# Projected keys copied out of PSUM once as f32 by ScalarE, with the remainder made by GpSimd

## What is computed

```python
kv = cond @ wkv.T + bkv                       # cond: 1500 x 256 per sequence
k, v = jnp.split(kv, 2, axis=-1)              # 16 heads of 16
attn = softmax(einsum('bnhd,bmhd->bhnm', q, k) * scale)
o = einsum('bhnm,bmhd->bnhd', attn, v)
out = qdq(o) @ qdq(wp).T + bp
```

## Time and profile before

| | us |
|---|---|
| median of 3 runs (lowest to highest) | 856.81 (855.29 to 857.29) |
| the profiled execution: its own time | 855.01 |
| the profiled execution: span from first to last instruction | 853.2 |
| PE busy | 772.5 (91%) |
| DVE busy | 638.0 (75%) |
| ACT busy | 510.9 (60%) |
| POOL busy | 296.4 (35%) |

### The profile page before, as it was taken

The page is one execution under the profiler, slowest core; times in us unless marked ns, Lnnn a source line. Parts: engine busy times, 40 slices in busy tenths (PEclk is TensorE's granted clock), DMA queues, the critical chain, the costliest instruction groups (busy, mean ns, idle before and its releaser), DMA issues.

```text
span 853.2 us, 30042 instructions
## 1 busy us (share of the span) xinstructions
PE 772.5 (91%) x12379; PEld 582.2 (68%) x12379; DVE 638.0 (75%) x1234; ACT 510.9 (60%) x1084; POOL 296.4 (35%) x366
## 2 busy tenths in 40 slices
PE   4689989999998999999899999999897799999996
PEld 2356666566666666666666666666665589999995
DVE  5877667777787879778787878877774735688887
ACT  2346666566576666666665666566654543777772
POOL 4263226232812461264217322722350003134232
PEclk9899999999999999999999999999999999999999
DMA  7366655454555556555555554645476975766653
GB/s 228 90 176 177 183 131 162 132 160 138 168 145 155 165 152 183 160 152 163 165 153 148 153 172 136 178 129 159 138 200 173 306 259 160 225 190 207 213 135 98
DMA packets 91380, 143.27 MB, mean 168 GB/s; under 512 B 11423, under 2 KB 79583, under 8 KB 87918
## 3 DMA queue, kind: packets, MB, share of 16 engines
q1 hardware_dynamic: 87742, 136.74, 53.8%
q0 software_dynamic: 3504, 4.62, 2.8%
HBM read 101.60 MB, written 39.68 MB: 166 GB/s over the span
## 4 chain that ended last, share of the span: by engine, by line
PE 62%; DVE 13%; ACT 10%; DMA 7%; issue 5%; SPq 2%; POOL 1%; DVEq 0%; POOLq 0%; ACTq 0%
PE ps L1655 14%; PE ps L1648 11%; PE ps L1967 7%; PE ps L1729 7%; PE ps L1707 6%; DVE negmax L522 4%; PE ps L2001 3%; DMA sums<-y_sb,g_token 3%; DMA k_st<-k_dram 3%; ACT pT L1437 3%; ACT k_front L1410 3%; PE ps L1671 3%; DVE k_front L516 3%; PE ps L1772 2%; PE ps L1988 2%
## 5 line engine op out<-in xcount | busy, mean ns | idle before, releaser
L522 DVE TENSOR_REDUCE negmax<-ps 112x1 f32<-112x1500 f32 x121 | 207.4, 1714 | 36.7 <-PE ps L1671 36.6
L1437 ACT ACTIVATE pT<-ps 125x448 f32<-125x448 f32 x384 | 195.6, 546 | 26.6 <-PE ps L1707 23.0
L1261 POOL TENSOR_TENSOR ctx_lo<-ctx_raw,ctx_hi 128x250 f16<-128x250 f32 x188 | 119.3, 666 | 177.8 <-DVE ctx_hi L507 177.8
L1707 PE MATMUL ps<-qbd,k_st 97*128 97x112 f16 x1536 | 128.2, 215 | 16.9 <-ACT pT L1437 8.9
L1707 PEld LDWEIGHTS ps<-qbd,k_st 97*128 97x128 f16 x1536 | 91.5, 99 | 73.1 <-ACT pT L1437 20.2
L1393 ACT COPY v_sb<-ps 125x512 f32<-125x512 f32 x96 | 56.3, 587 | 82.4 <-PE ps L1655 82.4
L516 DVE SCALAR_TENSOR_TENSOR k_front<-ps,bk_sb,k_front 128x500 f16<-128x500 f32 x80 | 58.8, 735 | 61.1 <-ACT k_front L1410 61.1
L1729 PE MATMUL ps<-pT,v_sb 125*17 125x56 f32 x6144 | 92.4, 216 | 8.5 <-issue 8.4
L1729 PEld LDWEIGHTS ps<-pT,v_sb 125*17 125x17 f32 x6144 | 80.6, 99 | 27.8 <-issue 16.1
L1410 ACT ACTIVATE k_front<-ps,bk_sb 128x500 f16<-128x500 f32 x80 | 54.3, 678 | 61.4 <-PE ps L1648 61.4
L1655 PE MATMUL ps<-wkv_hi,ctx_hi 128*125 128x256 f16 x384 | 76.4, 280 | 10.7 <-DVE k_front L516 9.2
(11 more groups left out here) (263 smaller groups left out, 1495.6 us busy)
## 6 DMA issues: line engine op xcount, KB each, us to landing
k_st<-k_dram SPq DMA_DIRECT2D x288, 125.0 KB, 3.0
w_sb<-w SPq DMA_DIRECT2D x25, 1024.0 KB, 5.0
ctx_raw<-ctx_T SPq DMA_DIRECT2D x48, 500.0 KB, 4.1
k_dram<-k_front SPq DMA_DIRECT2D x80, 250.0 KB, 2.7
xs<-zeros SPq DMA_DIRECT2D x28, 260.0 KB
w_sb<-w SPq DMA_DIRECT2D x8, 512.0 KB, 5.2
k_dram<-k_back SPq DMA_DIRECT2D x16, 250.0 KB, 2.9
xg<-xs SPq DMA_DIRECT2D x21, 130.0 KB, 4.1
```

Source lines behind the costliest of these rows:

```text
L522: V.tensor_reduce(negmax[0:QW], ps[0:QW, BANK_S:BANK_S + CHUNKS, 0:MC], AX.XY, ALU.max, negate=True).then_inc(max_done, 1)
L1261: last = nc.gpsimd.tensor_tensor(ctx_lo[:, k, c2, a], ctx_raw[:, k, c2, a], ctx_hi[:, k, c2, a], ALU.subtract)
L1437: nc.scalar.activation(pT[0:MT, (PAIRS * b + p) % 3, TPC * g:TPC * g + TPC], ps[0:MT, BANK_T + n % 2, 0:TPC * QW].rearrange("p (t n) -> p ...
L1707: last = mm(ps[:, BANK_T + n % 2, QW * i:QW * i + QW], k_st[:, j, p, a:a + P], qbd[:, j, p].rearrange("p h s -> p (h s)"), start=True, sto ...
```

## The change

ScalarE now reads the PSUM bank once, adds the bias and writes the key as f32 into one of two new buffers, `k_full`. This instruction frees the bank. A second ScalarE instruction rounds it to f16 (it waits for the first one's semaphore, `unit_out`). GpSimd subtracts in two halves of 250 columns and raises `k_lo_done`, for which the store waits; for the first batch alone the subtraction stays on VectorE. The six two-part buffers become four, used in turn, and ScalarE waits before it writes a buffer again. `load_keys` of unit 6 is issued directly behind its own store (its completion is waited for) and no longer behind unit 8's store. GpSimd's `iteration` gets a `k_lo_step` for every key unit, and three waits in `qbd_step` change.

```diff
             def unit_step(b, par, u):
                 c, g = UNIT[u]
                 if g in KEYS:
-                    i = key_place(c, g)
-                    dve.wait_ge(unit_done, UNITS * b + u + 1)
-
-                    dve.wait_ge(k_hi_done, len(KEY_UNITS) * b + KEY_UNITS.index(u) + 1)
-                    V.scalar_tensor_tensor(k_two[i][:, 1], ps[:, BANK_KV, 0:MC], bk_sb[:, g:g + 1], k_two[i][:, 0],
-                                           ALU.add, ALU.subtract).then_inc(unit_out, 1)
+                    n = key_number(b, u)
+
+                    dve.wait_ge(k_hi_done, n + 1)
+                    V.tensor_tensor(k_two[:, n % 4, 1], k_full[n % 2], k_two[:, n % 4, 0], ALU.subtract).then_inc(k_lo_done, 1)
...
-                    if units_on:
-                        for u in unit_slots(slot):
-                            unit_step(b + 1, 1 - j, u)
...
                         if u == 0:
                             load_keys(b - 1, j, KEY_UNITS[-1])
-                        else:
+                        elif u != 8:
                             load_keys(b, 1 - j, KEY_UNITS[KEY_UNITS.index(u) - 1])
+                        if u == 6:
+                            load_keys(b, 1 - j, u)
...
+            def k_lo_step(b, u):
+
+                n = key_number(b, u)
+                pool.wait_ge(k_hi_done, n + 1)
+                if n == len(KEY_UNITS):
+                    pool.wait_ge(k_lo_done, n)
+                for half in range(2):
+                    a = slice(MC // 2 * half, MC // 2 * half + MC // 2)
+                    last = nc.gpsimd.tensor_tensor(k_two[:, n % 4, 1, a], k_full[n % 2][:, a], k_two[:, n % 4, 0, a], ALU.subtract)
+                last.then_inc(k_lo_done, 1)
...
             def iteration(it, t_before):
-                ctx_lo_step(2 * it + 1, 1, 1)
+                b = 2 * it + 1
+                ctx_lo_step(b, 1, 1)
+                k_lo_step(b, 0)
+                k_lo_step(b, 2)
                 if it > 1:
                     scatter(it - 2)
                 if it > 0:
                     pool.wait_ge(b_oq_done, it)
                 kbd_step(it + 1)
...
             def k_hi_step(b, u):
 
                 c, g = UNIT[u]
-                i = key_place(c, g)
-                if b > 0:
-
-                    act.wait_ge(*stored(b - 1, u))
+                n = key_number(b, u)
                 act.wait_ge(unit_done, UNITS * b + u + 1)
-                nc.scalar.activation(k_two[i][:, 0], ps[:, BANK_KV, 0:MC], ACT.Identity,
-                                     bias=bk_sb[:, g:g + 1]).then_inc(k_hi_done, 1)
+                if n >= 2:
+
+                    act.wait_ge(k_lo_done, n - 1)
+                nc.scalar.activation(k_full[n % 2], ps[:, BANK_KV, 0:MC], ACT.Identity, bias=bk_sb[:, g:g + 1]).then_inc(unit_out, 1)
+                if n >= 4:
+
+                    act.wait_ge(*stored(n - 4))
+                act.wait_ge(unit_out, UNITS * b + u + 1)
+                copy(k_two[:, n % 4, 0], k_full[n % 2]).then_inc(k_hi_done, 1)
```

More of the change, by code:

```diff
@@ L161, in decoder_layer @@
         wkv_lo = sb("wkv_lo", [P, CH, 2 * D], F16)
-        k_front = sb("k_front", [P, 5, 2, MC], F16)
+        k_two = sb("k_two", [P, 4, 2, MC], F16)
+        k_full0 = sb("k_full0", [P, MC])
         sb("behind_k_front", [P, 8], F32)
@@ L168, in decoder_layer @@
         k_st = sb("k_st", [KA, 2, PAIRS, M + 4], F16)
-        k_back = sb("k_back", [P, 2, MC], F16)
+        k_full1 = sb("k_full1", [P, MC])
         sb("behind_keys", [P, 616])
@@ L220, in decoder_layer @@
         b_oqT = a_t2[:, D:D + P].bitcast(BF16).rearrange("p (c n) -> p c n", c=CH)
-        k_two = [k_front[:, n] for n in range(5)] + [k_back]
+        k_full = [k_full0, k_full1]
         staging = pT[:].rearrange("p a m n -> p (a m n)")
@@ L273, in decoder_layer @@
         k_hi_done = sem("k_hi_done")
+        k_lo_done = sem("k_lo_done")
         unit_out = sem("unit_out")
@@ L434, in key_place, with key_number, stored @@
             return CH * c + g
-        def stored(b, u):
-            n = KEY_UNITS.index(u)
-            return k_out[n % 2], 16 * (len(KEY_UNITS) // 2 * b + n // 2 + 1)
+        def key_number(b, u):
+            return len(KEY_UNITS) * b + KEY_UNITS.index(u)
+        def stored(n):
+            return k_out[n % 2], 16 * (n // 2 + 1)
         def loaded(b):
@@ L1082, in store_keys @@
                 c, g = UNIT[u]
-                i = key_place(c, g)
-                sp.wait_ge(unit_out, UNITS * b + u + 1)
+                i, n = key_place(c, g), key_number(b, u)
+                sp.wait_ge(k_lo_done, n + 1)
                 if not (isinstance(b, int) and b == 0):
                     sp.wait_ge(k_in[g], loaded(b - 1))
-                sp.dma_start(k_dram[i], k_two[i]).then_inc(stored(b, u)[0], 16)
+                sp.dma_start(k_dram[i], k_two[:, n % 4]).then_inc(stored(n)[0], 16)
                 for dst, src in between:
@@ L1094, in load_keys @@
                 i = key_place(c, g)
-                sp.wait_ge(*stored(b, u))
+                sp.wait_ge(*stored(key_number(b, u)))
                 for r, part in enumerate(KEY_PARTS[c]):
@@ L1173, in _ @@
                     load_keys(B - 2, 0, KEY_UNITS[-1])
-                else:
+                elif u != 8:
                     load_keys(B - 1, 1, KEY_UNITS[KEY_UNITS.index(u) - 1])
+                if u == 6:
+                    load_keys(B - 1, 1, u)
             load_keys(B - 1, 1, KEY_UNITS[-1])
@@ L1289, in qbd_step @@
                     pool.wait_ge(st_done, CHUNKS * PAIRS * (2 * t + j - 1))
-                if j == 1:
+                if j == 1 and (h == 1 or t == 0):
                     pool.wait_ge(qbd_done, 8 * t + 4 + 2 * h)
+                elif j == 1:
+                    pool.wait_ge(k_lo_done, 2 * len(KEY_UNITS) * t + len(KEY_UNITS))
+                elif h == 0 and not first:
+                    pool.wait_ge(k_lo_done, 2 * len(KEY_UNITS) * t + len(KEY_UNITS) - 1)
                 elif first and h == 0:
@@ L1330, in iteration @@
                 kbd_step(it + 1)
-                ctx_lo_step(2 * it + 1, 1, 2)
-                ctx_lo_step(2 * it + 2, 0, 0)
+                ctx_lo_step(b, 1, 2)
+                k_lo_step(b, 5)
+                k_lo_step(b, 6)
+                k_lo_step(b, 8)
+                ctx_lo_step(b + 1, 0, 0)
                 if t_before is not None:
                     b_rstd_step(t_before)
-                ctx_lo_step(2 * it + 2, 0, 1)
+                k_lo_step(b, 11)
+                ctx_lo_step(b + 1, 0, 1)
+                k_lo_step(b + 1, 0)
+                k_lo_step(b + 1, 2)
                 rstd_step(it + 1)
-                ctx_lo_step(2 * it + 2, 0, 2)
+                ctx_lo_step(b + 1, 0, 2)
+                k_lo_step(b + 1, 5)
+                k_lo_step(b + 1, 6)
+                k_lo_step(b + 1, 8)
                 qbd_step(it + 1, 0, 0)
-                ctx_lo_step(2 * it + 3, 1, 0)
+                ctx_lo_step(b + 2, 1, 0)
                 qbd_step(it + 1, 0, 1)
+                k_lo_step(b + 1, 11)
                 for h in range(2):
@@ L1369, in _ @@
             ctx_lo_step(B - 1, 1, 1)
+            k_lo_step(B - 1, 0)
+            k_lo_step(B - 1, 2)
             scatter(TILES - 3)
             ctx_lo_step(B - 1, 1, 2)
+            k_lo_step(B - 1, 5)
             b_rstd_step(TILES - 2)
+            for u in (6, 8, 11):
+                k_lo_step(B - 1, u)
             scatter(TILES - 2)
```

1 line of the change is left out of this document (removed).

## The result

| | before | after |
|---|---|---|
| median of the runs (lowest to highest) | 857.05 (855.29 to 857.64) | 884.56 (883.33 to 885.79) |
| the profiled execution: own time, span | 855.01, 853.2 | 885.79, 883.9 |
| granted TensorE clock over the span | 0.989 | 0.979 |
| PE busy | 772.5 | 785.7 |
| PE's waits, all their rows added | 73.9 | 90.3 |

The change makes the kernel 3.2% slower: ratio 1.0324 (1.0303 to 1.0346), 27.5 us. PE busy and PE's waits rise by 13.2 and 16.4 us, together 29.6 of the 30.7 us by which the two spans differ.

The account below looks back on a forecast made before the run. TensorE, busy 91% with an in-order queue, bounds the kernel, and ScalarE has no slack where TensorE waits for it. Costs of 33.2 (ScalarE) and 6.2 (GpSimd) less 19.5 gained give +19.9 us: 876, range 863 to 890.

Parts of the forecast that it names:

- The sum: Whole kernel: 33.2 + 6.2 - 19.5 = +19.9 us on the profiled 855.0, giving 874.9; 876 was forecast.
- The rounding stands in front of the `qbd` copy and is paid there: ScalarE, even slots: rounding delays the next slot's `qbd` copy, 0.65 us in full places, 0.56 in slots 5 and 11.
- Its sum: ScalarE's added rounding: 30.6 us in seven pairs plus 2.6 in the last projecting batch, together 33.2 us.
- `a_step` 3 behind `kbd_step`: Start of a pair: unit 2's remainder on GpSimd delays `kbd_step`; TensorE waits 1.25 us in 5 pairs, 6.2 us.
- The gain of 19.5 us: TensorE's waits taken as gone: 11.2 us for VectorE's remainder (bank freed earlier) and 8.3 us for keys (earlier load).
- The hidden rounding: Faster rival: TensorE finds other work while ScalarE rounds, or the copy costs little; 842 us, 12%.
- the break-even of 0.25 us a place: Deciding point for the hidden rounding: (19.5 - 6.2) / 53, the rounding's cost a place.
- The last block of the second half: Slower rival: unit 11's load, behind unit 0's store, comes late; TensorE stands 1.5 us in 7 pairs; 886, 12%.
- The third block: Slower rival: unit 6's keys are not loaded earlier, so the 8.3 us of waits stay; 883, 8%.
- GpSimd's port: Slower rival: added GpSimd instructions hold up VectorE through shared SBUF ports, 9.5 us more; 884, 7%.
- What would show it: Signs: remainder waits gone, `qbd` and exponential waits from 15 to 45 us or more, rounding 0.60 to 0.62, pair 83 to 84.

## Why the prediction was right

The forecast, 876 with a range of 863 to 890, holds the 884.6, and the sign is right; that the size is nearly right is in part luck, since two terms were wrong against each other. (The sum itself is 874.9 + 1.8 = 876.7, and its bounds and rivals leave out the 1.8.) Step by step:

- *The rounding stands in front of the `qbd` copy and is paid there.* Right, and shown three ways: by the marks in slots 3, 7, 9, 13 and 15, by the second copy (another 0.51 us a place), and by taking it away from there (the loss is gone). The instruction takes 0.608 us, and a place 0.69 with the wait for its own semaphore, against 0.61 and 0.65.
- *Its sum.* Mis-sized. The forecast was 33.2; the rows give some 28: the waits for `qbd`, for the exponentials and the marks of slot 7 go from 17.7 to 45.4 us (10.1 to 12.6 of them for exponentials, all lines). TensorE had about 0.14 us of slack in slots 3, 9 and 15, and in slots 5 and 11 it waits 0.2 to 0.3 us where I forecast 0.56. Alone, without the dependence, the copy costs 22.6.
- *`a_step` 3 behind `kbd_step`.* Right, smaller: 4.3 us more in four pairs, for the 6.2 in five, and the time is 4.1 us less when it is taken away.
- *The gain of 19.5 us.* This is the step that failed, though the rows seem to bear it out: 11.2 us of waits for the remainder and 5.6 of 8.3 for keys are gone. As time, the bank by itself is worth nothing that can be measured (856.8, at most some 2.7 us by its interval), and the loads 4.2 us. I took a wait that disappears as time that is gained. What takes the bank's time instead stays open: in that trace the "issue" waits are 12.0 us longer, but they are nearly as long in kernels that keep the waits for the remainder (last section).
- *The sum.* Right by terms that cancel: prices of 39.4 were nearer 32 (28 and 4.3), and gains of 19.5 nearer 5, if the two add up. In the waits alone the forecast of +19.9 stands against a measured +16.4; the 13.2 us of longer PE busy time, restarts and a lower clock, had no term.
- *Rivals.* The hidden rounding: no, the break-even of 0.25 us a place was passed by far. The last block of the second half: once, 2.1 and 0.6 us in the last pair, where a weight load stands in front. The third block: earlier in the changed kernel. GpSimd's port: no price here (waits for VectorE's row 0.7 us), but see below.
- *What would show it.* The waits on ACT came to 37.7 us by name and to 44 with the marks of slot 7 (said: 45 or more), the rounding to 0.61. A pair was to take 83 to 84 us: four of seven do or lie near; two, at clock 0.98, take 87.

## What to carry to other kernels

A copy put on an engine that is busy for 60% can cost nearly its full length where that engine's next instruction is one that TensorE waits for (here 0.55 to 0.69 us a place in five of seven slots, for 0.61 us of work); before anything else, look whether it can stand an instruction or two later, since here that gave back 26 us, 4 of them by the order on GpSimd. A wait that is taken away is not a gain until it is known what TensorE would wait for next: leave the waiting work out in one experiment, and count that. When a sum comes out right, test its terms one at a time.

## What the runs showed of the hardware

**Most waits that nothing releases come behind a load of instructions.** The "issue" waits of 0.5 us or more are eight in the kernel before and fourteen in the one without remainders. Each of them ends 2 to 3.5 us after the start of one 16 KB packet on the queue that carries instructions, and there is no second such packet in the 8 us before. For the wait that ends at 449.61 and the one that ends at 450.57 these are, by the quarter microsecond (446.50 to 446.75 in the kernel before, 447.25 to 447.50 without remainders; queue, packets, MB, share):

```profile
q8 instruction: 1, 0.02, 42.2%
```

```profile
q8 instruction: 1, 0.02, 46.5%
```

They come at the same matmuls in each kernel, but their lengths differ. At the 85th matmul above it is 1.15 us also with one more cast on ScalarE, and 1.98 with the loads' order alone:

```profile
468.80 0.38 PE L1734 MATMUL ps<-pT,v_sb 125*17 125x56 f32 x11 [1.15 <-issue]
```

```profile
455.25 0.38 PE L1733 MATMUL ps<-pT,v_sb 125*17 125x56 f32 x11 [1.98 <-issue]
```

All "issue" waits come to 22.3 us in the first of these two kernels (some 4 of them slot 7's marks) and to 22.2 in the second, as against 24.1 without the remainders, and both keep most of the waits for the remainder (9.0 and 10.5 us). So it is not shown that the bank's gain went into them, and how much they differ between executions of one kernel was not measured. That the packets cause the waits is inferred from these 22 cases; no run changed the packets. Three of them, of 2.19, 1.75 and 1.97 us, stand right before the clock falls in the kernel without remainders (0.51 granted from 450.7 to 454.0). By the Trainium skill, Runtime: NRT & Kernel Launch (Instruction fetch mechanics), instructions are refilled in blocks of 16 KiB, which agrees with 99 packets and 1.62 MB, and the cost is mostly hidden; here the eight waits of the kernel before alone come to 9.3 us, and the measurement decides.

**The clock and the time go together.** In 70 executions of the kernel before, those at a granted clock of 0.989 to 0.993 took as little as 851.7 us, those at 0.977 to 0.981 up to 863.1; a line through them falls by 5.5 us for each 0.01. The line is this kernel's own: the one with the rounding behind the third group took 858.3 us at a mean of 0.976. In the changed kernel TensorE went to the lower of its two levels (1.2 GHz) behind idle stretches such as the 0.91 us in slot 7 of two pairs, but not of the other four:

```profile
252.57 0.36 PE L1748 MATMUL ps<-qbd,k_st 97*128 97x112 f16 x4 [0.91 <-issue]
...
253.30 0.43 PE L1696 MATMUL ps<-wkv_hi,ctx_hi 128*125 128x256 f16 x2
253.53 0.63 PE L1696 MATMUL ps<-wkv_lo,ctx_hi 128*125 128x256 f16 x2
```

Two such matmuls take 0.38 us elsewhere in this trace and 0.63 here; the granted clock from 254 to 256 is 0.50.

**GpSimd can hold VectorE for several instructions.** In the kernel with the rounding behind the third group, where `kbd_step` and a remainder follow each other without a gap, VectorE's cast of a context chunk (0.68 us in the median) takes more than 4.5 us in five of 48 cases; DVE's timeline at the longest, and POOL's:

```profile
226.05 5.53 DVE L512 CAST ctx_hi<-ctx_raw 128x1000 f16<-128x1000 f32 x1
...
226.38 4.03 POOL L1274 TENSOR_TENSOR a_kbd<-a_qkT,hmask 128x512 f32<-128x512 f32 x4
230.38 1.70 POOL L1340 TENSOR_TENSOR k_two<-k_full,k_two 128x250 f16<-128x250 f32 x2
```

By the Trainium skill, SBUF — State Buffer (Who interferes with whom), the second to issue waits for the whole instruction of the first. The trace goes further: the cast starts ahead of `kbd_step` and ends at 231.58, behind all four of its instructions and within the remainder's two. In the changed kernel, where the remainder stands ahead of the scatter, no such cast takes more than 1.41 us, and in the kernel before none more than 1.33. TensorE waited 1.52 us for VectorE's row there.
